# Recommender head on one core: weights brought by another queue, first tile bank by bank, small layers between the head's passes

## The reference

```python
all_embed = jnp.concatenate([users_emb_w[users], items_emb_w[items]], axis=1)
h = jax.nn.relu(all_embed @ w1.T + b1)
h = jax.nn.relu(h @ w2.T + b2)
cross = jax.nn.one_hot(items, NUM_ITEMS, dtype=h.dtype)
head_in = jnp.concatenate([cross, h], axis=1)
return jax.nn.sigmoid(head_in @ w_head.T + b_head)
```

## Time and profile before

| | before |
|---|---|
| median of 3 runs | 66.62 us (66.48 to 66.84) |
| span of the profiled execution, first to last instruction | 65.9 us |
| PE busy | 56.0 us, 85% of the span |
| DVE, ACT, POOL busy | 43.0, 40.3, 31.2 us |
| bytes moved by DMA | 21.85 MB, mean 332 GB/s |

### The profile page before, as it was taken

One profiled execution on the slowest core, in us unless ns is written; L12 is line 12 of the kernel. 1 busy time (PEld: TensorE's weight loads), 2 busy tenths in 40 slices (PEclk: granted clock), 3 DMA queues, 4 the chain that ended last, 5 costly groups with the idle time before them and its releaser, 6 DMA issues.

```text
span 65.9 us, 958 instructions
## 1 busy us (share of the span) xinstructions
PE 56.0 (85%) x284; PEld 44.9 (68%) x284; DVE 43.0 (65%) x111; ACT 40.3 (61%) x91; POOL 31.2 (47%) x38
## 2 busy tenths in 40 slices
PE   1999909799999999999999999999999999993000
PEld 1344207388888888888888888888888878881000
DVE  3811666134558987978879797887978879966000
ACT  0623931424256787777878768787876878978000
POOL 4287688688688678768768868800000000000000
PEclk9999998555599999999999999999999999999955
DMA  0489998998989899999999999999999999999940
GB/s 0 53 321 291 298 350 257 222 343 259 222 283 303 336 382 401 392 406 409 401 410 414 400 426 411 410 413 415 410 402 395 419 404 401 390 346 346 372 145 9
DMA packets 8367, 21.85 MB, mean 332 GB/s; under 512 B 1580, under 2 KB 2476, under 8 KB 8364
## 3 DMA queue, kind: packets, MB, share of 16 engines
q0 software_dynamic: 2816, 10.77, 46.7%
q1 hardware_dynamic: 4972, 10.29, 41.1%
q10 hardware_dynamic: 576, 0.76, 3.8%
HBM read 11.56 MB, written 10.24 MB: 331 GB/s over the span
## 4 chain that ended last, share of the span: by engine, by line
PE 73%; DMA 11%; ACT 2%; DVE 2%; POOL 2%; issue 2%
PE acc L359 47%; DMA rows<-user_rows,idx 8%; PE ps_h L355 6%; PE acc L387 3%; PE acc L390 3%; PE acc L388 3%; PE ps_x L340 3%; PE ps_h L346 3%; DMA idx<-pairs 3%; PE ps_h L345 3%; PE acc L385 2%; POOL rows L181 2%; ACT rows L310 1%; DVE rows L244 1%; PE acc L355 1%
## 5 line engine op out<-in xcount | busy, mean ns | idle before, releaser
L244 DVE TENSOR_TENSOR rows<-acc,rows 128x625 f32<-128x625 f32 (+2 forms) x35 | 25.8, 749 | 5.3 <-PE acc L359 3.2
L310 ACT ACTIVATE rows<-rows 128x625 f32<-128x625 f32 (+2 forms) x35 | 23.3, 678 | 0.9 <-DVE rows L244 0.9
L181 POOL DMA_INDIRECT rows<-item_rows,idx x16 | 15.3, 954 | 6.0 <-issue 4.6
L185 POOL DMA_INDIRECT rows<-user_rows,idx x16 | 15.3, 955 | 4.9 <-issue 4.9
L359 PE MATMUL acc<-bias_parts,bias_sel 128*128 128x512 f32 (+1 forms) x42 | 11.2, 373 | 0.0
L359 PE MATMUL acc<-w_hid_hi,h2T_lo 128*128 128x512 f32 (+1 forms) x39 | 10.5, 376 | 0.0
L296 ACT ACTIVATE h1T<-ps_h,b_sb 128x128 f32<-128x128 f32 x16 | 5.9, 368 | 7.1 <-PE ps_h L346 6.6
L359 PE MATMUL acc<-w_hid_hi,h2T_hi 128*128 128x512 f32 (+1 forms) x39 | 10.0, 365 | 0.0
L300 ACT ACTIVATE h2T_hi<-ps_h,b_sb 128x128 fp32r<-128x128 f32 x15 | 5.5, 369 | 7.1 <-PE ps_h L355 7.1
L359 PE MATMUL acc<-w_hid_lo,h2T_hi 128*128 128x512 f32 (+1 forms) x39 | 9.6, 354 | 0.0
L227 DVE CAST embT<-ps_x 128x128 fp32r<-128x128 f32 x16 | 4.7, 292 | 5.5 <-PE ps_x L340 5.4
(11 more groups left out here) (39 smaller groups left out, 58.1 us busy)
## 6 DMA issues: line engine op xcount, KB each, us to landing
probs<-rows SPq DMA_DIRECT2D x20, 312.5 KB
probs<-rows SPq DMA_DIRECT2D x3, 625.0 KB
probs<-rows SPq DMA_DIRECT2D x6, 256.0 KB
w_hid_f<-w_hiddenT ACTq DMA_DIRECT2D x1, 625.0 KB
rows<-item_rows,idx POOLq DMA_INDIRECT x16, 5.9
rows<-user_rows,idx POOLq DMA_INDIRECT x16, 5.9
probs<-rows SPq DMA_DIRECT2D x2, 113.0 KB
probs<-rows ACTq DMA_DIRECT2D x1, 113.0 KB
```

The costliest lines, as they stand in the source:

```text
L181: nc.gpsimd.indirect_dma_start(out=rows[:, at + UD:at + ROW], out_offset=None, in_=item_rows, in_offset=bass.IndirectOffsetOnAxis(ap=idx[: ...
L185: nc.gpsimd.indirect_dma_start(out=rows[:, at:at + UD], out_offset=None, in_=user_rows, in_offset=bass.IndirectOffsetOnAxis(ap=idx[:, 2 * ...
L244: nc.vector.tensor_tensor(logits(t, c, n), acc[t % SLOTS][:, c:c + n], logits(t, c, n), ALU.add).then_inc(s_sum, 1)
L310: nc.scalar.activation(logits(t, c, n), logits(t, c, n), ACT.Sigmoid).then_inc(s_prob, 1)
```

## The change

What it does, part by part:

- The start. POOL issues the load of the head's weights, ahead of the identity matrix and the gathers. The zeroing of the identity goes to DVE. The two halves of `w1T` are issued by SP and by ACT, the head's bias by ACT. `b1` and `b2` come as two rows of 128 floats; PE transposes them into `ps_h`, DVE copies them to `b12_sb`.
- The warm-up. 3 matmuls of 512 columns in place of 6, then 4 of 128 columns after the first bank of the weights has been split by ACT and 3 after the second.
- Tile 0. Its layer 2 goes to `ps_x`. The order on PE around its banks changes, each bank waits for its own part of `w_hid_lo`, and T(1), L1(1) stand between the banks.
- The loop on PE: L1(t+1) moves from before hi(t) to between hi(t) and hi-lo(t). T(t+2) stays before lo(t).
- The loop on DVE: `copy_embT` moves to the front, and `split_emb(t+2)` from between the two adds to behind both.
- The loop on ACT: `relu_1(t+1)` moves behind `sigmoid(t-1, 0)`, and `relu_2(t+1)` behind `sigmoid(t-1, 1)`.
- The end: bank 0 of tile 14 goes ahead of L1(15); on DVE `split_h2(14)` goes behind the first add of tile 13.

```diff
-WARM = 6
+WARM = 3
+WARM_SHORT = (4, 3)
...
-            sp.dma_start(bias_f[:], bias_v).then_inc(s_bhead, 16)
-            for half in range(2):
-                sp.dma_start(w1T_f[half * K1:(half + 1) * K1, :], w1T).then_inc(s_w1, 16)
+            sp.dma_start(w1T_f[0:K1, :], w1T).then_inc(s_w1, 16)
...
-            nc.gpsimd.memset(ident[:], 0.0).then_inc(s_zero, 1)
+            pool.dma_start(w_hid_f[:], w_hiddenT).then_inc(s_hidden, 16)
...
+            nc.vector.memset(ident[:], 0.0).then_inc(s_zero, 1)
...
+            dve.wait_ge(s_b12_T, 1)
+            nc.vector.tensor_copy(b12_sb[:], ps_h[:, 0:2]).then_inc(s_b12_sb, 1)
...
             for t in range(2, LAST - 1):
-
+                copy_embT(t + 1)
                 add_part(t - 1, 0)
-                if t + 2 < TILES:
-                    split_emb(t + 2)
                 split_h2(t)
                 add_part(t - 1, 1)
-                if t + 2 < TILES:
-                    copy_embT(t + 2)
+                split_emb(t + 2)
+            copy_embT(LAST)
+            add_part(LAST - 2, 0)
             split_h2(LAST - 1)
-            add_rows(LAST - 2)
+            add_part(LAST - 2, 1)
...
-            act.dma_start(w_hid_f[:], w_hiddenT).then_inc(s_hidden, 16)
+            act.dma_start(w1T_f[K1:2 * K1, :], w1T).then_inc(s_w1, 16)
+            act.dma_start(bias_f[:], bias_v).then_inc(s_bhead, 16)
+            act.dma_start(b12_rows[0:1, :], b1.rearrange("(a p) -> a p", a=1)).then_inc(s_b12, 16)
+            act.dma_start(b12_rows[1:2, :], b2.rearrange("(a p) -> a p", a=1)).then_inc(s_b12, 16)
...
-            for t in range(2, LAST):
-
+            for t in range(2, LAST - 2):
+                sigmoid(t - 1, 0)
                 relu_1(t + 1)
-
+                sigmoid(t - 1, 1)
+                relu_2(t + 1)
+            for t in (LAST - 2, LAST - 1):
                 sigmoid(t - 1, 0)
+                relu_1(t + 1)
                 relu_2(t + 1)
                 sigmoid(t - 1, 1)
...
+            pe.wait_ge(s_b12, 32)
+            nc.tensor.transpose(ps_h[:, 0:2], b12_rows[:], ident[0:2, 0:2]).then_inc(s_b12_T, 1)
+            for bank, count in enumerate(WARM_SHORT):
+                pe.wait_ge(s_hid_hi, bank + 1)
+                warm_up(count, P)
             transpose(0)
...
+                    hi_pass(t, s)
+                    next_layer_1(t + 1)
+                    hi_lo_pass(s)
+                    layer_2(t + 1)
+                    transpose(t + 2)
+                    lo_pass(t, s)
+            bank_head(LAST - 1, 0)
             next_layer_1(LAST)
-            bank_head(LAST - 1, 0)
+            bank_head(LAST - 1, 1)
             layer_2(LAST)
```

More of the change, by code:

```diff
@@ L107, in rec_head_kernel @@
         s_b12 = sem("s_b12")
+        s_b12_T = sem("s_b12_T")
+        s_b12_sb = sem("s_b12_sb")
         s_hidden = sem("s_hidden")
@@ L295, in relu_1 @@
                 act.wait_ge(s_l1, t + 1)
-                nc.scalar.activation(h1T[:], ps_h[:, 0:P], ACT.Relu, bias=b1_sb[:]).then_inc(s_h1, 1)
+                nc.scalar.activation(h1T[:], ps_h[:, 0:P], ACT.Relu, bias=b12_sb[:, 0:1]).then_inc(s_h1, 1)
             def relu_2(t):
@@ L377, in lo_pass, with bank_bias, bank_hi, bank_lo @@
                 one_pass(s, h2T_lo[s][:], w_hid_hi, False, True).then_inc(s_acc, 1)
-            def bank_head(t, i):
+            def bank_bias(t, i):
                 s = t % SLOTS
                 c, n = chunks[i]
-                if t >= SLOTS:
-                    pe.wait_ge(s_sum, parts_until(t - SLOTS))
-                    nc.tensor.matmul(acc[s][:, c:c + n], bias_sel[:], bias_parts[:, c:c + n], start=True, stop=False)
+                pe.wait_ge(s_sum, parts_until(t - SLOTS))
+                nc.tensor.matmul(acc[s][:, c:c + n], bias_sel[:], bias_parts[:, c:c + n], start=True, stop=False)
+            def bank_hi(t, i):
+                s = t % SLOTS
+                c, n = chunks[i]
                 pe.wait_ge(s_h2_hi, t + 1)
                 nc.tensor.matmul(acc[s][:, c:c + n], h2T_hi[s][:], w_hid_hi[:, c:c + n], start=False, stop=False)
+                if t == 0:
+                    pe.wait_ge(s_hid_lo, i + 1)
                 nc.tensor.matmul(acc[s][:, c:c + n], h2T_hi[s][:], w_hid_lo[:, c:c + n], start=False, stop=False)
+            def bank_lo(t, i):
+                s = t % SLOTS
+                c, n = chunks[i]
                 pe.wait_ge(s_h2_lo, t + 1)
@@ L391, in bank_head, with warm_up @@
                                  start=False, stop=True).then_inc(s_bank_acc, 1)
+            def bank_head(t, i):
+                if t >= SLOTS:
+                    bank_bias(t, i)
+                bank_hi(t, i)
+                bank_lo(t, i)
+            def warm_up(count, cols):
+                for _ in range(count):
+                    nc.tensor.matmul(acc[0][:, 0:cols], warm_pe[:, 0:P], warm_pe[:, 0:cols], start=True, stop=True)
             pe.wait_ge(s_warm_pe, 1)
-            for _ in range(WARM):
-                nc.tensor.matmul(ps_x[:], warm_pe[:, 0:P], warm_pe[:], start=True, stop=True)
+            warm_up(WARM, BANK)
             pe.wait_ge(s_ident, 1)
+            pe.wait_ge(s_b12, 32)
[3 more added lines that the diff above has]
+                warm_up(count, P)
             transpose(0)
-            pe.wait_ge(s_w1_parts, 2)
             pe.wait_ge(s_const, 4)
             pe.wait_ge(s_bias_row, 32)
+            one_pass(0, bias_sel[:], bias_parts, True, True, chunks[:-1])
+            pe.wait_ge(s_w1_parts, 2)
+            layer_1(0)
             bias_pass(0)
-            layer_1(0)
-            bias_pass(1, chunks[:-1])
             pe.wait_ge(s_w2, 16)
             layer_2(0, second_layer(0))
+            bias_pass(1)
+            bank_hi(0, 0)
+            pe.wait_ge(s_h2, 1)
             transpose(1)
-            pe.wait_ge(s_h1, 1)
+            bank_lo(0, 0)
+            bank_hi(0, 1)
             layer_1(1)
-            bank_head(0, 0)
+            bank_lo(0, 1)
+            bank_hi(0, 2)
+            bank_lo(0, 2)
             layer_2(1)
-            bank_head(0, 1)
+            hi_pass(1, 1)
             transpose(2)
-            bias_pass(1, chunks[-1:])
-            bank_head(0, 2)
-            def small_beside_head(t, s):
-                next_layer_1(t + 1)
-                hi_pass(t, s)
-                hi_lo_pass(s)
-                layer_2(t + 1)
-                transpose(t + 2)
-                lo_pass(t, s)
-            small_beside_head(1, 1)
+            hi_lo_pass(1)
+            next_layer_1(2)
+            lo_pass(1, 1)
+            layer_2(2)
+            transpose(3)
             with pe.Fori(1, LAST // 2) as i:
```

38 lines of the change are left out of this document (16 added, 22 removed).

## The result

The changed kernel took 69.13 us (median of 4 runs, 68.75 to 70.78), beside 66.69 us (66.48 to 66.84, 4 runs) for the kernel before on the same chip. The ratio is 1.0346, with a 95% interval of 1.0298 to 1.0393: slower by 3.5%. The ratio and its interval leave out executions in a slower state of the chip, here the one of 70.78 us, so they are not the quotient of the medians. The forecast was 66.9 us, in a range of 65.2 to 68.2; the time lies above the range.

What follows compares the result with a forecast made beforehand. PE and the DMA engines were taken as two near bounds. Last store at 61.06 + 1.4 + 0.3 = 62.8, plus 3.1 and 0.4, gave a span of 66.3; plus 0.6 or 0.7, about 66.9 us, range 65.2 to 68.2.

Steps and rivals of the forecast that it cites:

- the anchor: From span to time: the median of the runs is 0.7 us longer than the span, so 66.3 becomes about 66.9.
- The clock, -2.7 us: Start, from tile 0's landing to lo(1): PE's clock holds its upper level, saving 2.7 us of 10.1.
- The second rival: Start: the clock falls as it did, lo(1) starts at 18.0; time 68.3 us, slower; chance 0.25.
- Tile 0, -1.5 us: Start: with the weights issued earlier, tile 0's gather lands at 7.9 us, 1.5 us sooner; ends 0 and -1.5.
- The third rival: Start: POOL's first DMA is slow or starved, gathers start a microsecond or more later; 67.8 us; chance 0.10.
- The loop, the step that decides: Loop: the new order lengthens each tile from 2.84 to 3.22 us; twelve tiles at +0.38 cost 4.6 us.
- The DVE ring: Loop: lo pass, both adds, split_emb, transpose and next lo pass form a closed ring of 3.22 us a tile.
- The second ring: Loop: lo, first add, first sigmoid, relu_1, L2, T, lo; about 3.0 us, hidden behind the ring through DVE.
- The cap by the gathers: Early loop: tile 6's user rows land at 25.2, so lo(4) starts no earlier than 26.0; lo(13) at 55.0, +1.4 us.
- The end: After lo(13): split_h2(14) waits for tile 13's first add, delaying tile 14's first bank; +0.3 us, ends 0 and 0.6.
- SP's last wait: Behind the last store: 4.4 us falls to 3.1, as an earlier first store leaves less to drain; ends 2.7 and 4.4.

Runs made afterwards that it cites:

- before, again: The kernel before, unchanged, profiled a second time: 66.63 us, one run.
- c1 to c3: On a slow chip (kernel before 96.39 us): before with tiles 3 to 11 stored whole, before with stores held, new start mended with old loop; 97.06, 96.76, 99.32 us.
- a2: The kernel before with the loop and end of the changed kernel: 68.84 us, ratio 1.029 to the kernel before.
- a3: The kernel before with the head's weights issued by POOL as its first work, in place of ACT: 67.17 us, ratio 1.0041.
- d1: The kernel before with SP's first store held until tile 5's gathers have landed: 68.65 us, ratio 1.0208.
- d2: The changed kernel's start with the head's bias issued by SP, and the loop and end of the kernel before: 66.77 us, ratio 0.9975.
- b2: The changed kernel with the head's bias issued by SP again, in place of ACT: 68.10 us, one run.
- a4: The changed kernel with DVE's loop and end in the order of the kernel before: 68.55 us, one run.
- a5: The changed kernel with ACT's order in loop and end, and L1's place on PE, as before: 68.82 us, one run.

## Why the prediction was wrong

The step that failed is the anchor, the addition of 0.7 us to the span, where 1.8 belong: with it the same sum would have given 66.3 + 1.8 = 68.1 us. With it failed the gains of the start (-2.7 and -1.5 us), which were counted from an execution slower than those timed. That the loop lengthens was right, with one ring of two. Several other terms came out near the measured ones by luck, and are named below.

**The anchor.** "The median of the runs is 0.7 us longer than the span" tied two different executions together. Of one and the same execution, time less span is 1.8 us: 68.94 - 67.1 in the changed kernel, 66.63 - 64.8 in before, again. This step alone is 1.1 to 1.2 us of the 2.2 by which the time missed the forecast. The span came out at 67.1, against 66.3.

**The clock, -2.7 us.** The clock does hold in the changed kernel, as forecast, but it holds in before, again, too. There was nothing to win. From the landing of tile 0 to lo(1) I had 10.1 us from the execution profiled at first; from tile 0's cast at 9.00 the ordinary one takes 7.7. The second rival (the clock falls) named the right sign and a time of 68.3, 0.8 below the measured, for a wrong reason: apart from that first one, the clock fell before the end of PE's work in no profile but those of c1 to c3. What made it fall there was not found.

**Tile 0, -1.5 us.** Forecast: rows at 7.9. They were cast at 8.24, against 9.00 in before, again. But the six other profiles with the new start have that cast at 8.44 to 9.24, and those without it (a2, a3, d1) at 8.94 to 9.13, so the gain is about 0.4 us in the mean and in some executions nothing. What there was of it went in the wait for the bias rows, a move I had listed in the change and not followed to its reader. lo(1) starts at 17.41 to 17.69 in the five profiles of the new start with the bias on ACT, and at 16.61 and 16.66 in the two with it on SP (d2, b2). The weights through POOL alone gave nothing (a3): the 0.9 us by which I had them issued earlier were 0.39. In the whole new start ACT's first split comes at 5.60 (5.58 to 5.92 in its seven profiles), against 6.13 in before, again, and 5.2 in the forecast; which part of the change brings that no run separates. The third rival (POOL's DMA slow or starved) is out by a3, in which tile 0's rows came no later. That agrees with the strict reading of the Trainium skill, "SBUF — State Buffer", section "SBUF: two separate sides": DVE's clearing of buffers is not among the operations said to keep GpSimd from writing descriptors.

**The loop, the step that decides.** The DVE ring was right in its parts. It measures 3.07 us, and 3.16 in three turns, not 3.22, and 0.13 of the difference is one term: the handover from DVE to PE is 0.14 us on a PE in motion, not the 0.27 of the earlier trace rows, taken on one that had stood still. The second ring, "about 3.0 by similar steps and hidden behind the first", was worked out too loosely. It is 3.07 as well, and a4 and a5 show that either alone would have cost the same.

**The cap by the gathers.** lo(4) starts at 27.26 and lo(13) at 55.24, close to the 55.0 of the forecast, but by luck: lo(4) comes 1.26 us later than the 26.0 of the cap, and the nine turns from there are shorter by 0.11 each in the mean (3.11 for 3.22). lo(1) started two microseconds later than forecast, and the sign I had named, a cast of tile 6's embedding that waits for its gather, isn't there. PE waits for no gather in tiles 4 to 13 of the changed kernel. In before, again, it does: lo(4) starts at 27.22 there, level with the changed kernel. Its lead from the shorter tiles is thus only what comes after: 2.28 us at lo(13), nine tiles of about 0.25.

**The end.** From lo(13) to the last store: 7.96 us, against 7.44 in the earlier trace rows and 7.42 in before, again, so +0.5 where I took +0.3. The wait for `h2T_lo` before the last matmul of tile 14's first bank is there, 0.40 us. SP's last wait was 3.4 us, where I took 3.1, again by luck. My term came from a first store near 13.4 us that would leave 1.2 us less to drain; it left at 15.29, no earlier than the 14.95 of before, again. What shortens the wait is that PE ends so late that the DMA engines have run dry: the last store lands 3.5 us after its issue.

**Readings and sums.** The DMA strip of the earlier trace rows has an 8 in slices 9, 11 and 13 (counted from 0) and its last 9 in slice 37, so "nine tenths or more from slice 9 to slice 38" was too much. From 13.4 to 16.92 us it moved 343, 259 and 222 GB/s, not 222 to 283. The point at which the second rival decides is 26.0 - 3 x 3.22 = 16.3, not 16.6, and the third rival's time is 67.9, not 67.8. None of these changes the argument.

In sum, by ordinary profiles: +0.7 at lo(1), nothing left of that at lo(4), +2.28 at lo(13), +2.82 at the last store, -0.54 in the last wait, +2.28 in the span, and +2.44 in the medians.

## What to carry to other kernels

Before a term is built on one profile, tie the profile to the timed runs: if its own time isn't given, a stretch at the lower clock is a reason to doubt that it stands for them. A sum over a ring always gives the distance that the passes have; to say which ring binds, look for the handover without slack, or open one ring after the other. When instructions are put in another order on several engines, close every ring from one pass to the next and add each up with the same care; undoing one of two equal rings shows nothing, and that is the sign of the second. With PE and the DMA engines both near full, time saved on PE ends in a longer wait for the last store, while time lost on PE past the DMA engines' slack is paid.

## What the runs showed of the hardware

- The granted clock of one and the same kernel fell in one profiled execution (slices 7 to 10 of the earlier trace rows) and held in the next (0.921 and 0.988 in the mean).
- Gathers are slower beside stores: the user rows issued near 16.9 us landed 3.8 us later with no store under way, and 6.4 later beside stores. Whether the gathers slow the stores no run shows.
- The same load can take different times to issue: that of the head's bias takes 0.40 us as SP's second and 0.92 as ACT's second. On ACT it cost 0.75 us at lo(1) (changed against b2).
- Handovers in the loop: 0.05 us from the end of DVE's subtraction to the transpose's weight load and 0.14 to the matmul behind the transpose, and 0.05 from the end of `relu_1` (48.67) to L2 (48.72).
